# The sums of a windowed softmax: from ScalarE's exponentials to one VectorE reduction over each block

## The chip, the cores and the metric

The kernel runs on one core of a Trainium2 chip. The metric is the device time of one execution, in microseconds (us).

## The reference

Two blocks follow each other on a state of 4 x 1024 tokens of 128 channels. This case is about the second half of the first block: six layers, each a local attention (16 heads of 64, windows of 32 tokens that look back one window) and a feed-forward part. Cut to the attention:

```python
q = q * cos * scale + rotate_half(q) * sin * scale
k = k * cos * inv + rotate_half(k) * sin * inv
...
sim = jnp.einsum('bhwie,bhwje->bhwij', bq, bk2) * QK_SCALE
sim = jnp.where(mask, -jnp.finfo(sim.dtype).max, sim)
attn = jax.nn.softmax(sim, -1)
out = jnp.einsum('bhwij,bhwje->bhwie', attn, bv2)
```

For each token and head the softmax runs over 64 keys. Before this stage stand a full attention with another score function, behind it a recurrence and a mixture of experts; the change touches neither.

## The kernel before, in words

`local_layers` works through 96 units (6 layers x 16 units of 256 tokens), pipelined over several steps: in one step each engine does pieces of up to six units, `at(1)` (the youngest) to `at(6)`. Every engine has its own fixed list of calls in a function `step`, written out by hand, and runs it in order; engines meet through semaphores only. The steady part is a loop whose body holds two steps (`for odd in range(2)`), so units come in pairs; I call the step that ends in the loop's jump and what follows it the odd one, the other the even one.

A unit has two blocks of 128 tokens, x = 0 and x = 1. For a block, with tokens on the 128 partitions, the steps are:

- `scores` (PE, L775 and L782) writes 16 heads x 64 keys to a PSUM pair, the mask among them.
- `maxima` (DVE, L1148) takes the maximum of each head, and `loc_ebias` (L1150) turns it into the bias of the exponential.
- `exponentials(x, hp)` (ACT, L990) has one ACTIVATE for each of 8 heads, 128x64, with a bias and a scale from SBUF, and writes `loc_probs`. Its `accum_out` adds up the 64 numbers of a head into `loc_total`. There are four such groups of eight in a unit.
- `reciprocals(x)` (DVE, L1157) forms `loc_recip` = 1/`loc_total`, 128x16.
- `probs_across`, `probs_out`, `weighted`, `outputs` (PE L804, ACT L1008, PE L819, DVE L1166) transpose, multiply by the values and scale by `loc_recip`.

Around these lie the rotary products (`rotate_cos` L1090 and `rotate_sin` L1099 on DVE, after ACT's squares L972; the halves of `loc_msin` are swapped by DMAs that SP issues, and POOL adds them, L691, into `loc_ks` and `loc_qr`), the norms of the heads (`norms`, `norms_out` L979, `norms_across` L757, `norms_in` L1108, and `newton`, ten small operations of DVE on lines 91 to 95 that make `loc_rnorm`), the spreading of the key norms (`widen` L1127 into `loc_rk_wide`, `spread` PE L765, `scale_keys` DVE L1138), and the second half's LayerNorm (`centre` L1187, `ln_squares` ACT L1022, `ln_var` PE L854, `ln_rstd` DVE L1195 and again lines 91 to 95, `ln_spread` PE L862).

DVE's list for a step, where it matters here: `norms_in`, `reciprocals(0)`, `newton`, `rotate_cos(0)`, `widen(0)`, `rotate_sin(0)`, ..., `maxima(0, 0)`, `reciprocals(1)`, `scale_keys(1)`, and in the next step `maxima(0, 1)`, `centre`, `outputs(1)`, `ln_rstd`. ACT's: `norms_out`, `exponentials(1, 0)`, `square(0)`, `exponentials(1, 1)`, ..., `outputs_out(0)`, `exponentials(0, 0)`, `ln_squares`. PE's: `out_projection`, `project(1)`, `spread(0)`, `weighted(0)`. In that list of PE, `spread(0)` waits for two things: `widen(0)`, and, since it writes the PSUM pair from which `exponentials(1, 1)` read, for these exponentials. `weighted(0)` writes the pair that `rotate_sin(0)` reads. POOL's second `rotated` call of a unit follows `scale_keys(1)`.

Of the kernel before, what the change touches and what calls it, by code (L numbers as in the profile page):

```python
# [11 lines left out]
ALU = mybir.AluOpType  # L12
ACT = mybir.ActivationFunctionType
AX = mybir.AxisListType
# [38 lines left out]
def semaphores(nc, ctx, prefix):  # L53

    made = []

    def sem(name):
        made.append(ctx.enter_context(nc.semaphore(prefix + name)))
        return made[-1]

    return made, sem
# [57 lines left out]
def count(n, per=1, k=1):  # L119

    return START + per * n + k


def after(eng, sem, n, per=1, k=1):

    if not isinstance(n, int) or per * n + k > 0:
        eng.wait_ge(sem, count(n, per, k))
# [330 lines left out]
def local_layers(nc, const, t):  # L458

    ctx = ExitStack()  # L460
    with ctx:
        sb = lambda s, sh, dt=F32: ctx.enter_context(nc.sbuf_tensor("loc_" + s, sh, dt))
        pb = lambda s, sh: ctx.enter_context(nc.psum_tensor("loc_" + s, sh, F32))
        sems, sem = semaphores(nc, ctx, "loc_")
        x, ident, mean_w = const["x"], const["ident"], const["mean_w"]
# [22 lines left out]
        rnorm = [sb(f"rnorm{i}", [P, 2, 2 * HEADS]) for i in range(2)]  # L488
        rk_wide = sb("rk_wide", [P, HEADS * DH])
        mx, ebias, total, recip = ([sb(f"{s}{i}", [P, HEADS]) for i in range(2)] for s in ("mx", "ebias", "total", "recip"))  # L490
        probs = [sb(f"probs{i}", [P, PAIRS, 2, 2 * WIN]) for i in range(2)]
# [23 lines left out]
        mx_ready, ebias_ready, exp_ready, recip_ready = sem("mx_ready"), sem("ebias_ready"), sem("exp_ready"), sem("recip_ready")  # L515
# [3 lines left out]
        mean_ps, xc_ready, lsq_ready, var_ps, rstd_ready = sem("mean_ps"), sem("xc_ready"), sem("lsq_ready"), sem("var_ps"), sem("rstd_ready")  # L519
        lnspread_ps, xn_ready, h_ready = sem("lnspread_ps"), sem("xn_ready"), sem("h_ready")  # L520
        ff_ps, gelu_ready, hidden_ready, y_ps, xa_done = sem("ff_ps"), sem("gelu_ready"), sem("hidden_ready"), sem("y_ps"), sem("xa_done")
        fpar_ready = sem("fpar_ready")
        links, nlinks, vlinks = sem("links"), sem("nlinks"), sem("vlinks")
        passed = sem("passed")
        block = ctx.enter_context(nc.Block())
# [431 lines left out]
        def _(act):  # L957
# [23 lines left out]
            def exponentials(x, hp, u, b):  # L981
                if u is None:
                    return
                after(act, ebias_ready, u.n, 4, 2 * x + hp + 1)
                if hp == 0:
                    after(act, probsT_ps, u.n - 1, 2, x + 1)
                    after(act, recip_ready, u.n - 1, 2, x + 1)
                for p in range(PAIRS):
                    k, head = PAIRS * hp + p, HEADS + 2 * p + hp
                    ins = nc.scalar.activation(probs[x][:, p, hp, :], pairs[b][:, hp, p * 2 * WIN:(p + 1) * 2 * WIN], ACT.Exp, bias=ebias[x][:, k:k + 1],  # L990
                                               scale=rnorm[u.odd][:, x, head:head + 1], accum_out=total[x][:, k:k + 1])
                ins.then_inc(exp_ready, 1)

            def values_out(x, u, b):
# [44 lines left out]
            def step(at):  # L1039
                ln_squares(at(5))  # L1040
                square(2, at(2), 2)
                exponentials(0, 1, at(3), 1)
                values_out(0, at(3), 0)
                h_out(at(5))
                outputs_out(1, at(4), 1)
                gelus(0, at(5), 4)
                probs_out(0, at(3), 0)
                square(3, at(2), 1)
                values_out(1, at(3), 0)
                norms_out(at(2), 4)  # L1050
                exponentials(1, 0, at(3), 2)
                square(0, at(1), 1)
                exponentials(1, 1, at(3), 2)
                gelus(1, at(5), 3)
                square(1, at(1), 0)
                probs_out(1, at(3), 2)
                gelus(2, at(5), 3)
                outputs_out(0, at(3), 2)
                exponentials(0, 0, at(2), 1)
# [4 lines left out]
        def _(dve):  # L1064
# [88 lines left out]
            def reciprocals(x, u):  # L1153
                if u is None:
                    return
                after(dve, exp_ready, u.n, 4, 2 * x + 2)
                nc.vector.reciprocal(recip[x][:, :], total[x][:, :]).then_inc(recip_ready, 1)  # L1157

            def outputs(x, u, b):
# [65 lines left out]
            def step(at):  # L1225
# [13 lines left out]
                rotate_sin(3, at(2), 1)  # L1239
                norms_in(at(2), 4)  # L1240
                reciprocals(0, at(3))
                newton(at(2))
                rotate_cos(0, at(1), 1)
# [8 lines left out]
                widen(1, at(2))  # L1252
                maxima(0, 0, at(2), 1)
                reciprocals(1, at(3))
                scale_keys(1, at(2), 0)

# [358 lines left out]
def kernel_program(nc, t, out, phases=5):  # L1615
    ctx = ExitStack()
    with ctx:
        sb = lambda s, sh, dt=F32: ctx.enter_context(nc.sbuf_tensor(s, sh, dt))
        const = {
            "x": sb("x", [P, TOK]), "ident": sb("ident", [P, P]), "mean_w": sb("mean_w", [P, P]),  # L1620
            "mod": sb("mod", [P, 2 * 6 * BATCH]),
        }
        prepare(nc, const, t)
        if phases >= 1:
            theta_attention(nc, const, t)
        if phases >= 2:
            local_layers(nc, const, t)
        if phases >= 3:
            rwkv(nc, const, t)
        if phases >= 4:  # L1630
            mixture(nc, const, t, out)
        else:
            store(nc, const, out)
# [87 lines left out]
```

## Time and profile before

| | us |
|---|---|
| three runs | 5411.45, 5433.7, 5434.81 (median 5433.7) |
| the profiled execution, its own time | 5389.72 |
| its span, first to last instruction | 5387.8 |
| PE busy in the span | 4167.7 (77%) |
| DVE busy | 3552.1 (66%) |
| ACT busy | 3140.0 (58%) |
| POOL busy | 1080.8 (20%) |

The profiled execution took 5389.72 us, 0.8% less than the median of the three others; sums are made against it. The local layers take up about 81% of the span (560 to 4920 us). Busy shares say only that no engine is full; the pace comes from who waits for whom inside a step.

### The profile page before, as it was taken

The page shows a single profiled execution, that of the slowest core. Times are in us where ns is not written, and L with a number is a line of the kernel's source. Part 1 is how long each engine was busy: PE and PEld are TensorE (multiplying, and loading weights), DVE is VectorE, ACT ScalarE, POOL GpSimd, SP SyncE. Part 2 cuts the span into 40 slices and gives each one's busy share as a digit, 9 for nine tenths or more (in the row PEclk, how much of TensorE's full clock was granted, in tenths as well). Part 3 has the DMA queues.
Part 4 walks back from the last instruction along what each step waited for, and adds up shares of the span by engine and source line. Part 5 has one row for each costly group of instructions (what it writes and reads, how often), then busy time and mean ns, then how long its engine had stood idle before and what let it go on. Part 6 is the DMA issues. An engine that isn't in the chain of part 4 may idle for free. (4 is left out here: it accounts for less than half of the span.)

```text
span 5387.8 us, 176120 instructions
## 1 busy us (share of the span) xinstructions
PE 4167.7 (77%) x68250; PEld 2955.4 (55%) x68250; DVE 3552.1 (66%) x6841; ACT 3140.0 (58%) x8480; POOL 1080.8 (20%) x856
## 2 busy tenths in 40 slices
PE   5665688888888888888888888888888888885358
PEld 3443465555655656565556565556565656563124
DVE  4454576677676766676766677766766767774655
ACT  3332466666666766666666666666666666673123
POOL 0000222222222222222222222222222222220011
PEclk9776899999999999999999999999999999997579
DMA  0001233323333333333333333333333333330000
GB/s 24 0 0 38 68 77 71 73 69 89 76 72 72 73 79 82 72 72 70 81 77 77 73 72 73 84 81 72 69 72 81 85 72 74 71 81 11 0 9 12
DMA packets 138485, 337.32 MB, mean 63 GB/s; under 512 B 44880, under 2 KB 46032, under 8 KB 137552
## 3 DMA queue, kind: packets, MB, share of 16 engines
q1 hardware_dynamic: 137808, 326.67, 25.8%
q8 instruction: 622, 10.19, 0.9%
q14 instruction: 55, 0.45, 0.0%
HBM read 22.41 MB, written 2.10 MB: 5 GB/s over the span
## 5 line engine op out<-in xcount | busy, mean ns | idle before, releaser
L990 ACT ACTIVATE loc_probs<-loc_pair,loc_ebias,loc_rnorm 128x64 f32<-128x64 f32 x3072 | 1198.7, 428 | 13.4 <-DVE loc_ebias L1150 11.0
L738 PE MATMUL loc_pair<-loc_hs,loc_wqk 128*128 128x256 f32 x3072 | 795.5, 405 | 155.6 <-issue 152.3
L691 POOL TENSOR_TENSOR loc_ks<-loc_mcos,loc_swapped 128x1024 f32<-128x1024 f32 x192 | 452.1, 2355 | 1833.2 <-DVE loc_kr L1138 1345.6
L738 PEld LDWEIGHTS loc_pair<-loc_hs,loc_wqk 128*128 128x128 f32 x3072 | 589.3, 199 | 271.8 <-issue 170.6
L691 POOL TENSOR_TENSOR loc_qr<-loc_mcos,loc_swapped 128x1024 f32<-128x1024 f32 x192 | 452.6, 2357 | 1387.2 <-DMA loc_swapped<-loc_msin 1316.0
L990 ACT ACTIVATION_READ_ACCUMULATOR loc_probs<-loc_pair,loc_ebias,loc_rnorm 128x1 f32 x3072 | 704.5, 229 | 0.0
L1090 DVE SCALAR_TENSOR_TENSOR loc_mcos<-loc_pair,loc_scal,loc_tab 128x1024 f32<-128x1024 f32 x384 | 491.1, 1279 | 189.7 <-ACT loc_sq L972 170.0
L972 ACT ACTIVATE loc_sq<-loc_pair 128x1024 f32<-128x1024 f32 x384 | 395.8, 1031 | 336.1 <-PE loc_pair L738 336.1
L1148 DVE TENSOR_REDUCE loc_mx<-loc_pair 128x8 f32<-128x512 f32 x384 | 264.5, 689 | 466.6 <-PE loc_pair L782 458.4
L1099 DVE SCALAR_TENSOR_TENSOR loc_msin<-loc_pair,loc_scal,loc_tab 128x1024 f32<-128x1024 f32 x384 | 490.0, 1276 | 28.7 <-DMA loc_swapped<-loc_msin 27.4
L1001 ACT ACTIVATE loc_vodd<-loc_pair 128x1024 f32<-128x1024 f32 x192 | 196.9, 1026 | 410.4 <-DMA loc_veven<-loc_vodd 286.8
L782 PE MATMUL loc_pair<-loc_kr,loc_qr 64*32 64x64 f32 x24576 | 320.4, 226 | 137.7 <-issue 137.7
L782 PEld LDWEIGHTS loc_pair<-loc_kr,loc_qr 64*32 64x32 f32 x24576 | 272.1, 106 | 238.9 <-issue 236.2
L795 PE MATMUL loc_pair<-loc_wv,loc_hs 128*64 128x512 f32 x1536 | 401.8, 647 | 1.6 <-DVE loc_o L1166 1.4
L1166 DVE TENSOR_TENSOR loc_o<-loc_pair,loc_recip 128x512 f32<-128x512 f32 x384 | 246.3, 682 | 232.1 <-PE loc_pair L819 232.1
L819 PE MATMUL loc_pair<-loc_veven,loc_probsT 64*32 64x64 f32 x12288 | 315.3, 235 | 89.5 <-issue 82.0
L1008 ACT ACTIVATE loc_probsT<-loc_pair 128x1024 f32<-128x1024 f32 x192 | 195.9, 1020 | 317.4 <-PE loc_pair L804 317.4
L872 PE MATMUL loc_one<-loc_h,loc_w 128*128 128x256 f32 (+1 forms) x1152 | 330.2, 411 | 31.7 <-ACT loc_h L1029 22.9
L819 PEld LDWEIGHTS loc_pair<-loc_veven,loc_probsT 64*32 64x32 f32 x12288 | 272.1, 109 | 148.3 <-issue 147.8
L839 PE MATMUL loc_one<-loc_oT,loc_wo 128*128 128x256 f32 x1536 | 350.1, 381 | 0.8 <-DVE loc_act_out L1211 0.4
L1015 ACT ACTIVATE loc_oT<-loc_pair 128x1024 f32<-128x1024 f32 x192 | 195.2, 1017 | 253.9 <-PE loc_pair L829 253.9
L1150 DVE SCALAR_TENSOR_TENSOR loc_ebias<-loc_mx,loc_rnorm 128x8 f32<-128x8 f32 x384 | 313.0, 815 | 13.2
(244 smaller groups left out, 7503.6 us busy)
## 6 DMA issues: line engine op xcount, KB each, us to landing
loc_swapped<-loc_msin SPq DMA_DIRECT2D x1536, 128.0 KB, 2.3
loc_veven<-loc_vodd SPq DMA_DIRECT2D x768, 64.0 KB, 2.0
loc_veven<-loc_vodd SPq DMA_DIRECT2D x384, 128.0 KB, 2.3
loc_wqk<-wqk_dram SPq DMA_DIRECT2D x12, 512.0 KB, 3.6
loc_wv<-wv_dram SPq DMA_DIRECT2D x6, 512.0 KB, 3.6
loc_wo<-wo_dram SPq DMA_DIRECT2D x6, 512.0 KB, 4.4
x<-xT_dram SPq DMA_DIRECT2D x1, 2048.0 KB, 7.4
loc_tab<-tables_dram SPq DMA_DIRECT2D x1, 2048.0 KB, 7.7
```

The lines of the kernel that those rows point to most:

```text
L691: nc.gpsimd.tensor_tensor(dst, mcos[i % 2][:, :], swapped[:, :], ALU.add).then_inc(rope_add, 1)
L738: ins = nc.tensor.matmul(pairs[b][:, p // 2, (p % 2) * UNIT:(p % 2 + 1) * UNIT], wqk[:, k, w:w + P], hs[u.odd][:, :], start=True, stop=True)
L782: ins = nc.tensor.matmul(pairs[b][WIN * w:WIN * w + WIN, hp, p * 2 * WIN:(p + 1) * 2 * WIN], qr[u.odd][part, p, at:at + WIN], kr[u.odd][pa ...
L795: ins = nc.tensor.matmul(pairs[b][hp * DH:(hp + 1) * DH, g, :], hs[u.odd][:, BLK * x + DH * g:BLK * x + DH * g + DH], wv[:, hp, :], start= ...
L819: ins = nc.tensor.matmul(pairs[b][WIN * w:WIN * w + WIN, hp, p * DH:(p + 1) * DH], probsT[part, p, WIN * w:WIN * w + WIN], v[part, w // 2, ...
L839: ins = nc.tensor.matmul(bank(b)[:, 0:UNIT], wo[:, p, :], oT[:, p, :], start=p == 0, stop=p == PAIRS - 1)
L872: ins = nc.tensor.matmul(bank(b)[0:FB[j], k * UNIT:(k + 1) * UNIT], w1[:, at:at + FB[j]], h[:, :], start=True, stop=True)
L972: nc.scalar.activation(sq[:, i, :], flat(b), ACT.Square).then_inc(sq_ready, 1)
L990: ins = nc.scalar.activation(probs[x][:, p, hp, :], pairs[b][:, hp, p * 2 * WIN:(p + 1) * 2 * WIN], ACT.Exp, bias=ebias[x][:, k:k + 1], sc ...
L1090: nc.vector.scalar_tensor_tensor(mcos[i % 2][:, :].rearrange("p (g t) -> p g t", g=4), flat(b).rearrange("p (g t) -> p g t", g=4), scal[u. ...
L1099: nc.vector.scalar_tensor_tensor(msin[:, :].rearrange("p (g t) -> p g t", g=4), flat(b).rearrange("p (g t) -> p g t", g=4), scal[u.odd][:, ...
L1150: nc.vector.scalar_tensor_tensor(ebias[x][:, k], mx[x][:, k], -1.0, rnorm[u.odd][:, x, HEADS:].rearrange("p (g y) -> p y g", y=2)[:, hp, : ...
```

## The change

The exponentials lose `accum_out`. `reciprocals(x)` first adds up `loc_probs` of the block, 128 partitions x 16 heads x 64, with one `tensor_reduce` of DVE into `loc_total`, waits for it by a new semaphore, and then takes the reciprocals. The wait of `exponentials(x, 0)` for the reciprocals of the unit before falls away.

```diff
@@ exponentials
                 if hp == 0:
                     after(act, probsT_ps, u.n - 1, 2, x + 1)
-                    after(act, recip_ready, u.n - 1, 2, x + 1)
                 for p in range(PAIRS):
                     k, head = PAIRS * hp + p, HEADS + 2 * p + hp
                     ins = nc.scalar.activation(probs[x][:, p, hp, :], pairs[b][:, hp, p * 2 * WIN:(p + 1) * 2 * WIN], ACT.Exp, bias=ebias[x][:, k:k + 1],
-                                               scale=rnorm[u.odd][:, x, head:head + 1], accum_out=total[x][:, k:k + 1])
+                                               scale=rnorm[u.odd][:, x, head:head + 1])
                 ins.then_inc(exp_ready, 1)
@@ reciprocals
                 after(dve, exp_ready, u.n, 4, 2 * x + 2)
+                nc.vector.tensor_reduce(total[x][:, :].rearrange("t (y g) -> t g y", y=2), probs[x][:, :, :, :], AX.X, ALU.add).then_inc(sum_ready, 1)
+                dve.wait_ge(sum_ready, count(u.n, 2, x + 1))
                 nc.vector.reciprocal(recip[x][:, :], total[x][:, :]).then_inc(recip_ready, 1)
```

On DVE, in the middle of a step, the reciprocals of block 0 stand between the reading of the norms and the ten operations of `newton`. Before:

```order
620 L1108 TENSOR_SCALAR loc_norm<-loc_one 128x4x4x2 x2
621 L1157 RECIPROCAL loc_recip<-loc_total 128x16
622 L91 TENSOR_SCALAR loc_rnorm<-loc_norm 128x64
623 L76 ISA
624 L93 SCALAR_TENSOR_TENSOR loc_ntmp<-loc_rnorm,loc_norm 128x64
```

and in the changed kernel (a line added and one taken away above make the numbers of some lines differ by one):

```order
628 L1107 TENSOR_SCALAR loc_norm<-loc_one 128x4x4x2 x2
629 L1156 TENSOR_REDUCE loc_total<-loc_probs 128x8x2
630 L1158 RECIPROCAL loc_recip<-loc_total 128x16
631 L91 TENSOR_SCALAR loc_rnorm<-loc_norm 128x64
632 L76 ISA
633 L93 SCALAR_TENSOR_TENSOR loc_ntmp<-loc_rnorm,loc_norm 128x64
```

The reduction stands ahead of `newton`, and all of `newton` moves back behind it. At the end of a step, between `maxima(0, 0)` and `scale_keys(1)`, the order before is this; there the reduction comes in ahead of L1157 in the same way, and ahead of `scale_keys(1)` (L1138):

```order
664 L1148 TENSOR_REDUCE loc_mx<-loc_pair 128x8
665 L1150 SCALAR_TENSOR_TENSOR loc_ebias<-loc_mx,loc_rnorm 128x8
666 L1157 RECIPROCAL loc_recip<-loc_total 128x16
667 L127 REGISTER_ALU
668 L1138 TENSOR_TENSOR loc_kr<-loc_ks,loc_pair 128x8x128
```

ACT's order stays; each of its exponentials writes one tile where it wrote two. Before, around the two groups of block 1 (first row) and the gelu behind them:

```order
273 L990 ACTIVATE loc_probs,loc_total<-loc_pair,loc_ebias,loc_rnorm 128x64 x16
274 L1036 ACT_TABLE_LOAD
275 L1036 ACTIVATE loc_gelu<-loc_one,loc_fpar 128x256
```

and now:

```order
273 L989 ACTIVATE loc_probs<-loc_pair,loc_ebias,loc_rnorm 128x64 x16
274 L1035 ACT_TABLE_LOAD
275 L1035 ACTIVATE loc_gelu<-loc_one,loc_fpar 128x256
```

No instruction of ACT changes its place.

## Rows read from the trace of the kernel before

**Rows 1.** The page's costliest groups: the exponentials and their accumulator reads (count, busy us, mean ns)

```profile
L990 ACT ACTIVATE loc_probs<-loc_pair,loc_ebias,loc_rnorm 128x64 f32<-128x64 f32 x3072 | 1198.7, 428 | 13.4 <-DVE loc_ebias L1150 11.0
...
L990 ACT ACTIVATION_READ_ACCUMULATOR loc_probs<-loc_pair,loc_ebias,loc_rnorm 128x1 f32 x3072 | 704.5, 229 | 0.0
```

**Rows 2.** Timeline of ACT, an even unit: start, duration, what

```profile
2548.60 0.40 ACT L990 ACTIVATE loc_probs<-loc_pair,loc_ebias,loc_rnorm 128x64 f32<-128x64 f32 x1
2548.90 0.19 ACT L990 ACTIVATION_READ_ACCUMULATOR loc_probs<-loc_pair,loc_ebias,loc_rnorm 128x1 f32 x1
2549.00 0.39 ACT L990 ACTIVATE loc_probs<-loc_pair,loc_ebias,loc_rnorm 128x64 f32<-128x64 f32 x1
```

**Rows 3.** Groups of instructions on DVE, shapes apart

```profile
L94 DVE TENSOR_TENSOR loc_ntmp<-loc_ntmp,loc_rnorm 128x64 f32<-128x64 f32 x288 | 82.1, 285 | 9.9
...
L442 DVE TENSOR_REDUCE att_mx<-att_theta 128x1 f32<-128x1024 f32 x32 | 39.0, 1220 | 1.1
```

**Rows 4.** PE's waits, 1000 to 4500 us: us in total, times, longest

```profile
PE loc_pair L765 <- ACT loc_probs L990: 58.4, 57, 1.1
PE loc_one L862 <- DVE loc_rstd L95: 55.3, 36, 2.3
PE loc_one L854 <- ACT loc_lsq L1022: 50.9, 39, 1.4
```

**Rows 5.** Timeline of DVE, the even unit of [rows 2]

```profile
2548.48 0.25 DVE L1157 RECIPROCAL loc_recip<-loc_total 128x16 f32<-128x16 f32 x1
...
2550.89 0.23 DVE L95 SCALAR_TENSOR_TENSOR loc_rnorm<-loc_ntmp,loc_rnorm 128x64 f32<-128x64 f32 x1
2552.95 1.28 DVE L1090 SCALAR_TENSOR_TENSOR loc_mcos<-loc_pair,loc_scal,loc_tab 128x1024 f32<-128x1024 f32 x1 [1.83 <-ACT loc_sq L972]
...
2554.75 1.28 DVE L1099 SCALAR_TENSOR_TENSOR loc_msin<-loc_pair,loc_scal,loc_tab 128x1024 f32<-128x1024 f32 x1
```

**Rows 6.** Timeline of POOL: the middle of an odd step, then of the even one

```profile
2505.69 2.36 POOL L691 TENSOR_TENSOR loc_qr<-loc_mcos,loc_swapped 128x1024 f32<-128x1024 f32 x1 [8.18 <-DMA loc_swapped<-loc_msin]
...
2551.01 2.36 POOL L691 TENSOR_TENSOR loc_qr<-loc_mcos,loc_swapped 128x1024 f32<-128x1024 f32 x1 [4.87 <-DMA loc_swapped<-loc_msin]
```

**Rows 7.** Timeline of POOL and DVE, another even unit

```profile
1465.04 2.35 POOL L691 TENSOR_TENSOR loc_qr<-loc_mcos,loc_swapped 128x1024 f32<-128x1024 f32 x1 [4.61 <-DMA loc_swapped<-loc_msin]
1465.17 2.30 DVE L95 SCALAR_TENSOR_TENSOR loc_rnorm<-loc_ntmp,loc_rnorm 128x64 f32<-128x64 f32 x1
```

**Rows 8.** Timeline of PE: five waits in a pair of units

```profile
2508.66 1.09 PE L765 MATMUL loc_pair<-ident,loc_rk_wide 128*128 128x128 f32 x8 [0.93 <-DVE loc_rk_wide L1127]
...
2531.72 0.43 PE L862 MATMUL loc_one<-ident,loc_rstd 128*128 128x128 f32 x2 [0.86 <-DVE loc_rstd L95]
...
2555.93 1.09 PE L765 MATMUL loc_pair<-ident,loc_rk_wide 128*128 128x128 f32 x8 [0.91 <-ACT loc_probs L990]
...
2559.10 0.24 PE L819 MATMUL loc_pair<-loc_veven,loc_probsT 64*32 64x64 f32 x1 [0.71 <-issue]
...
2572.24 0.61 PE L854 MATMUL loc_one<-mean_w,loc_lsq 128*128 128x1 f32 x4 [1.41 <-ACT loc_lsq L1022]
```

**Rows 9.** Timeline of DVE, the odd unit of [rows 6]

```profile
2506.85 1.75 DVE L1127 COPY loc_rk_wide<-loc_rnorm 128x1024 f32<-128x1024 f32 x1
...
2518.41 1.22 DVE L1138 TENSOR_TENSOR loc_kr<-loc_ks,loc_pair 128x1024 f32<-128x1024 f32 x1 [0.28 <-PE loc_pair L765]
...
2528.64 0.90 DVE L91 TENSOR_SCALAR loc_rstd<-loc_var 128x2 int32<-128x2 int32 x1
```

**Rows 10.** Timeline of POOL, behind the end of the odd unit's step

```profile
2527.16 2.35 POOL L691 TENSOR_TENSOR loc_ks<-loc_mcos,loc_swapped 128x1024 f32<-128x1024 f32 x1 [4.87 <-DMA loc_swapped<-loc_msin]
```

**Rows 11.** Timeline of DVE, the end of the even unit's step

```profile
2567.22 1.22 DVE L1138 TENSOR_TENSOR loc_kr<-loc_ks,loc_pair 128x1024 f32<-128x1024 f32 x1 [0.64 <-PE loc_pair L765]
...
2569.07 1.93 DVE L1150 SCALAR_TENSOR_TENSOR loc_ebias<-loc_mx,loc_rnorm 128x8 f32<-128x8 f32 x1
2570.92 0.41 DVE L1187 TENSOR_TENSOR loc_xc<-loc_xb,loc_one 128x256 f32<-128x256 f32 x1
```

More of the change, by code:

```diff
@@ L521, in local_layers @@
         ff_ps, gelu_ready, hidden_ready, y_ps, xa_done = sem("ff_ps"), sem("gelu_ready"), sem("hidden_ready"), sem("y_ps"), sem("xa_done")
-        fpar_ready = sem("fpar_ready")
+        fpar_ready, sum_ready = sem("fpar_ready"), sem("sum_ready")
         links, nlinks, vlinks = sem("links"), sem("nlinks"), sem("vlinks")
```

## The prediction

> **What bounds the kernel now.** I read the page first: PE is the busiest engine, but with pauses, and the exponentials and the reads of their accumulators head ACT's list [rows 1]. 3072 exponentials at 32 a unit are 96 units. Then I read PE's waits, since no engine is full and the pace is that of the engine that everybody follows. Over 3500 us, some 77 units, the waits that this change can touch are three [rows 4]: `spread(0)` (L765) waits 58.4 us for the exponentials that still read its PSUM pair, `ln_spread` (L862) waits 55.3 us for the LayerNorm's Newton steps, `ln_var` (L854) waits 50.9 us for the squares. The sum is 165 us, 2.1 us a unit and 4.7% of that time, so the removal of 700 us of accumulator reads cannot show in full. The timelines of ACT, DVE and POOL around these three waits say who is late for each, and the rest of this text stays there.
>
> **ACT: what is taken off.** An accumulator read lasts 229 ns in the mean [rows 1], but it starts 0.30 us after its ACTIVATE began and the next ACTIVATE starts 0.10 us after it [rows 2]: they overlap. Without it I expect the next ACTIVATE where the read stood, so 0.10 us for each, 0.8 us for a group of eight, about 3.1 us a unit, 0.3 ms of ACT time in all. Bounds: nothing, if an ACTIVATE needs its 0.40 us of pitch anyway, and 0.23 us each, the read's whole duration. The value in between is read from two starts, so I trust it. The Trainium skill, ScalarE: Activation LUTs, What ACT_TABLE_LOAD costs, gives 186 ns plus 93 ns for each pointer operand plus 0.833 ns a column, less 93 ns of overlap back to back, which would be an estimate of 0.33 us of pitch and a gain of 0.07 us instead of 0.10; the duration that it gives, 425 ns, agrees with the row's 428.
>
> **DVE: what is added.** 192 reductions of 128x1024. The nearest row is the reduction of the same size in the stage before, 1.22 us [rows 3]; with the step to the reciprocal that now waits for it, about 1.25 us, 240 us in all. Bounds: 1.1 and 1.5 us; the 16 heads of 64 could cost a little at each head's end.
>
> **Middle of a step.** In the even unit L1157 starts at 2548.48, the last operation of `newton` ends at 2551.12, and DVE then waits 1.83 us for ACT's squares before L1090 [rows 5]. The reduction seems to fit into this pause, all the more since the squares come 0.8 us earlier behind a shorter group. But POOL starts a sum at 2551.01 [rows 6], and another even unit shows what happens when `newton` is still running then: POOL starts at 1465.04, the operation of DVE that starts at 1465.17 takes 2.30 us in place of 0.23 and ends when POOL's ends [rows 7]. The mean of L94 on `loc_ntmp`, 285 ns for an operation that mostly takes 0.23, says that this is rare now: 288 x 0.055 us is 16 us, seven or eight catches of 2.1 us on this line. With 1.25 us put ahead of it, `newton` in this even unit would run from 2549.9 to 2552.4, so half of it falls behind POOL's start. Its sixth operation is in flight at 2551.1, or held until 2553.4, and four more follow at 0.26 us: end at 2554.5. L1090 comes at 2554.4 in place of 2552.95, and L1099 at 2556.2 in place of 2554.75. PE's `spread(0)` needs L1127, ready at 2556.3, and starts at 2556.4 in place of 2555.93 [rows 8], although the exponentials for which it waited now are done 1.6 us earlier. `weighted(0)` needs L1099's end, 2557.5: it starts at about 2557.7 where it could start at 2556.95 before, 0.75 us later. What ACT gives is lost here, since DVE, which was not late, becomes late. POOL's start varies against this step by some tenths, and in many units L1108 comes earlier than here, so I take 0.6 us for an even unit. Bounds: 0.8, and 0, since PE stops inside `weighted(0)` for 0.71 us with no releaser [rows 8], and if what it waits for there (its next code) doesn't come later too, this pause takes up the delay.
>
> The rule that bears on the reduction itself is in the Trainium skill, GPSIMD Engine Reference, Specifications: GpSimd and VectorE share SBUF interfaces, with contention for DVE instructions in a two-port mode or with two SBUF inputs. By it the reduction, with one SBUF input, isn't held and `newton` is; the trace agrees for `newton` [rows 7], and no row shows a reduction beside POOL. Were it held as well, nothing would change here, for at 2548.5 to 2549.7 POOL is idle.
>
> In the odd unit POOL starts later against the step, at 2505.69, and `newton`, which ended near 2503.8, ends near 2505.1: just free. L1127 is held by POOL there (1.75 us for a copy of 0.68) until POOL ends [rows 9, 6], and PE's `spread(0)` waits for it [rows 8]. An earlier start of that copy changes nothing while POOL ends when it does. I take -0.1 us for an odd unit.
>
> **End of a step.** The reduction also stands ahead of `scale_keys(1)`. In the even unit L1138 had waited 0.64 us for PE [rows 11], so it comes 0.6 us later. POOL's next sum waits for it, L1150 is held by that sum (1.93 us) and moves along, and L1187 ends at 2571.9 in place of 2571.33 [rows 11]. The squares L1022 came at 2571.74 behind `exponentials(0, 0)`, 0.5 us before PE's L854 at 2572.24 [rows 8]. Now the exponentials are done 0.8 us earlier and the centred rows 0.6 us later: L1022 starts at about 2571.9, 0.15 us late. In the odd unit L1138 had only 0.28 us of pause [rows 9], so it comes 1.0 us later, and with it the sum of POOL that waits for it and, after a swap by DMA, the next one, at 2527.16 [rows 10]. This one holds the LayerNorm's first Newton step: L91 at 2528.64 takes 0.90 us [rows 9]. Moved to 2528.1 it holds L91 until 2530.5, and PE's L862, which waits 0.86 us there [rows 8], waits 0.9 us longer. In units in which that sum started late already it would slide behind all ten steps (2 us) and the wait, 1.5 us in the mean (55.3 us in 36) [rows 4], would go. Between +0.9 and -1.5 I take +0.25, nearer to the unit I read, in which the sum would have to move 2.5 us to be out of the way.
>
> **The sum.** For a pair: 0.6 - 0.1 + 0.15 + 0.25 = 0.9 us. 48 pairs, of which about 45 run with all stages full: 40 us, 0.75%. On the profiled execution's own 5389.7 us that is 5430. The median of the three runs is 0.8% above that execution; with the same ratio it becomes 5474, and I give 5470. The PSUM and semaphore parts of the edit cost nothing: `exponentials(x, 0)` drops a wait that was long fulfilled, since its wait for `loc_ebias` stands behind the reciprocals in DVE's order.
>
> **Rivals.** *The sums are hidden and ACT's gain counts.* If POOL's sum came after `newton` in even units, `spread(0)` would start 0.9 us earlier (its whole wait, [rows 8]): -0.9 - 0.1 + 0.15 + 0.25 = -0.6 us a pair, -27 us, 5407. It decides at a start of POOL 1.4 us later against the step than in [rows 6]. Chance 0.10. *The LayerNorm slips free.* The odd unit's POOL sum moves behind the Newton steps in most units: at -1.5 us in four of five odd units and +0.9 in the rest, -1.0 us, a pair gets 0.6 - 0.1 + 0.15 - 1.0 = -0.35 us, -16 us, and with the first delay absorbed -0.95 us, -43 us: 5390 to 5418. It decides where this sum starts more than 1.8 us behind L91. For it, the 2.3 us of the longest wait [rows 4]; against it, L91's row. Chance 0.12. *Nothing to be measured.* PE's pause in `weighted(0)` takes up the 0.6 us: 0.3 us a pair, 13 us, 5447. Chance 0.22. *The odd unit is caught too.* `newton` ends at 2505.1 against POOL's 2505.69, 0.6 us of room; if reductions take 1.5 us or POOL comes earlier, L1090 and PE's `weighted(0)` come 0.6 us later there as well: 1.6 us a pair, 72 us, 5506. Chance 0.12. The forecast itself has 0.44.
>
> **How the numbers follow.** About 0.5% is what a measurement of this kernel can tell from no change. The forecast's own range, from 0.4 to 1.3 us a pair, is 5450 to 5493, and a third of it lies within 0.5%. Slower by over 0.5%: 0.30 + 0.12 + a little of the third rival, 0.45. Within: 0.35. Faster by over 0.5%: the first two where they go far, 0.20. The range for 8 in 10 reaches to 5405 below, into the faster cases, and to 5520 above, past the catch in both units.
>
> **What would show it.** ACTIVATE to ACTIVATE on the exponentials 0.29 to 0.30 us, and no accumulator read. The reduction at 1.2 us. L93, L94 and L95 on `loc_rnorm` and `loc_ntmp` with a mean near 0.3 to 0.5 us, one operation of 2.2 us in nearly every even unit; PE's L765 waiting for DVE in place of ACT; L1090 without its wait for the squares there. L862's wait longer, L854's about the same. I'm wrong if the step is bound elsewhere: if PE's waits without a releaser shrink by what I add, if POOL's sums move against `newton`, or if `ln_spread` loses its wait.

## The result and the profile after

| | before | after |
|---|---|---|
| median of the runs, us | 5434.26 (5411.45 to 5437.28, 4 runs) | 5551.59 (5537.94 to 5557.66, 4 runs) |
| the profiled execution, its own time | 5389.72 | 5537.94 |
| DVE busy | 3552.1 | 3922.8 |
| ACT busy | 3140.0 | 2868.5 |

The ratio is 1.0222, with an interval of 1.0188 to 1.0256: slower by 2.2%, where 0.7% had been forecast, and above the range. In the profiled executions the difference is 148 us, 3.1 us for each of the 48 pairs; the forecast's sum was 0.9.

Groups of instructions (count | busy us, mean ns | idle before, releaser), beside [rows 1] and [rows 3]:

```profile
L989 ACT ACTIVATE loc_probs<-loc_pair,loc_ebias,loc_rnorm 128x64 f32<-128x64 f32 x3072 | 952.7, 431 | 12.1 <-DVE loc_ebias L1149 9.8
...
L1156 DVE TENSOR_REDUCE loc_total<-loc_probs 128x16 f32<-128x1024 f32 x192 | 233.8, 1217 | 3.3
...
L94 DVE TENSOR_TENSOR loc_ntmp<-loc_ntmp,loc_rnorm 128x64 f32<-128x64 f32 x288 | 133.3, 463 | 9.9
L93 DVE SCALAR_TENSOR_TENSOR loc_ntmp<-loc_rnorm,loc_norm 128x64 f32<-128x64 f32 x288 | 96.9, 336 | 9.9
...
L95 DVE SCALAR_TENSOR_TENSOR loc_rnorm<-loc_ntmp,loc_rnorm 128x64 f32<-128x64 f32 x288 | 90.1, 313 | 9.9
```

The group of 3072 accumulator reads is gone, and the exponentials last as long as before each (431 ns, 428 before). The reductions cost 234 us of DVE. The three kinds of `newton` step are the same instructions as before, and L94 went from 285 to 463 ns in the mean: that is time in which they were held.

PE's waits from 1000 to 4500 us (us in total, times, longest), beside [rows 4]:

```profile
PE loc_pair L738 <- issue: 111.7, 37, 3.5
PE loc_pair L782 <- issue: 105.2, 70, 2.2
PE loc_pair L765 <- DVE loc_rk_wide L1126: 98.7, 98, 1.6
PE loc_pair L819 <- issue: 96.2, 58, 2.8
PE loc_one L862 <- DVE loc_rstd L95: 81.3, 37, 2.4
...
PE loc_one L854 <- ACT loc_lsq L1021: 57.9, 37, 1.6
```

`spread(0)` (L765) waited 58.4 us for ACT's exponentials and 24.6 for DVE, 83.0 together; it now waits 98.7 us, all for DVE. `ln_spread` (L862) waits 81.3 us where it waited 55.3. The pauses without a releaser inside `weighted(0)` (L819) were 70.5 us in 54 before and are 96.2 in 58.

The middle of a step, the even unit, in the timelines (start, duration, what, idle before): ACT, DVE, POOL, PE.

```profile
2712.18 2.52 ACT L989 ACTIVATE loc_probs<-loc_pair,loc_ebias,loc_rnorm 128x64 f32<-128x64 f32 x8
```

```profile
2708.50 1.22 DVE L1156 TENSOR_REDUCE loc_total<-loc_probs 128x16 f32<-128x1024 f32 x1
2709.75 0.25 DVE L1158 RECIPROCAL loc_recip<-loc_total 128x16 f32<-128x16 f32 x1
...
2711.12 2.42 DVE L94 TENSOR_TENSOR loc_ntmp<-loc_ntmp,loc_rnorm 128x64 f32<-128x64 f32 x1
...
2714.73 1.28 DVE L1089 SCALAR_TENSOR_TENSOR loc_mcos<-loc_pair,loc_scal,loc_tab 128x1024 f32<-128x1024 f32 x1 [0.15 <-issue]
2715.93 0.68 DVE L1126 COPY loc_rk_wide<-loc_rnorm 128x1024 f32<-128x1024 f32 x1
2716.53 1.28 DVE L1098 SCALAR_TENSOR_TENSOR loc_msin<-loc_pair,loc_scal,loc_tab 128x1024 f32<-128x1024 f32 x1
```

```profile
2711.10 2.36 POOL L691 TENSOR_TENSOR loc_qr<-loc_mcos,loc_swapped 128x1024 f32<-128x1024 f32 x1 [5.95 <-DMA loc_swapped<-loc_msin]
```

```profile
2716.67 1.09 PE L765 MATMUL loc_pair<-ident,loc_rk_wide 128*128 128x128 f32 x8 [1.47 <-DVE loc_rk_wide L1126]
...
2718.06 0.25 PE L819 MATMUL loc_pair<-loc_veven,loc_probsT 64*32 64x64 f32 x2 [0.30 <-DVE loc_msin L1098]
...
2721.95 0.24 PE L819 MATMUL loc_pair<-loc_veven,loc_probsT 64*32 64x64 f32 x1 [2.42 <-issue]
```

Eight exponentials take 2.5 us, about 0.3 us apiece from start to start (0.290 in the mean of all, 0.382 before), as forecast from [rows 2]; 0.33, the other estimate there, was too high. The reduction and the reciprocal put L94's second pass at 2711.12, just behind the start of POOL's sum at 2711.10, and that 0.23 us operation lasts 2.42. L1089 has lost its wait for the squares (1.83 us in [rows 5]), because it is late itself. All of that the prediction named. What it did not name is the last row: PE starts `weighted(0)` at 2718.06, stops near its end and resumes at 2721.95, after 2.42 us; the same pause was 0.71 us in [rows 8]. That was a short one: over 40 even units the pauses of L819 come to 1.64 us a unit before and 2.26 after.

The end of the odd unit's step, DVE, POOL and then PE, beside [rows 8 to 10]:

```profile
2783.76 2.22 DVE L95 SCALAR_TENSOR_TENSOR loc_rstd<-loc_vtmp,loc_rstd 128x2 f32<-128x2 f32 x1
```

```profile
2783.61 2.35 POOL L691 TENSOR_TENSOR loc_ks<-loc_mcos,loc_swapped 128x1024 f32<-128x1024 f32 x1 [5.60 <-DMA loc_swapped<-loc_msin]
```

```profile
2786.99 0.43 PE L862 MATMUL loc_one<-ident,loc_rstd 128*128 128x128 f32 x2 [2.31 <-DVE loc_rstd L95]
```

One Newton step of the LayerNorm is held for a whole sum of POOL, and `ln_spread` waits 2.31 us, where the unit shown before had a hold of 0.9 us and a wait of 0.86.

One unit can mislead, so I averaged the starts of some instructions over 40 even and 40 odd units of each trace, counted from the start of ACT's copy of the norms (L979). Times in us:

| | even: length | `newton` ends | L1098 starts (`rotate_sin(0)`) | `weighted(0)` starts / its last matmul | `ln_spread` | odd: length | `weighted(0)` starts | `scale_keys(1)` | `ln_spread` |
|---|---|---|---|---|---|---|---|---|---|
| before | 43.73 | 4.29 | 7.89 | 10.05 / 13.30 | 30.91 | 46.80 | 10.31 | 18.64 | 32.13 |
| after | 45.47 | 7.39 | 9.34 | 10.87 / 14.73 | 32.63 | 48.23 | 10.43 | 20.00 | 33.12 |
| `reciprocals(0)` early | 43.38 | 3.97 | 7.32 | 8.90 / 12.57 | 30.61 | 46.96 | 9.84 | 19.15 | 32.32 |
| both moved | 42.08 | 4.27 | 7.37 | 8.95 / 12.58 | 29.19 | 46.27 | 9.69 | 18.11 | 31.37 |
| both moved, accumulators kept | 43.69 | 4.19 | 7.89 | 10.05 / 13.26 | 30.94 | 46.66 | 10.26 | 18.49 | 31.86 |

The last three rows are experiments below. A pair got 1.74 + 1.43 = 3.2 us longer. In the even unit `weighted(0)` starts 0.82 us later, close to what I had worked out (0.75), but its last matmul comes 1.43 us later.

### The profile page after: what moved, and what is told of

It reads as the page before. It is cut to its first block and busy times, and to the rows that moved or that the text cites. A ratio compares the mean times of both kernels' runs of the same rounds, so it can differ in the third digit from the quotient of the medians.

```text
span 5536.0 us, 173241 instructions
## 1 busy us (share of the span) xinstructions
PE 4208.0 (76%) x68250; PEld 2977.0 (54%) x68250; DVE 3922.8 (71%) x7033; ACT 2868.5 (52%) x5408; POOL 1083.0 (20%) x856
## 5 line engine op out<-in xcount | busy, mean ns | idle before, releaser
L989 ACT ACTIVATE loc_probs<-loc_pair,loc_ebias,loc_rnorm 128x64 f32<-128x64 f32 x3072 | 952.7, 431 | 12.1 <-DVE loc_ebias L1149 9.8
L1089 DVE SCALAR_TENSOR_TENSOR loc_mcos<-loc_pair,loc_scal,loc_tab 128x1024 f32<-128x1024 f32 x384 | 490.8, 1278 | 44.6 <-issue 20.7
L1098 DVE SCALAR_TENSOR_TENSOR loc_msin<-loc_pair,loc_scal,loc_tab 128x1024 f32<-128x1024 f32 x384 | 489.9, 1276 | 37.1 <-DMA loc_swapped<-loc_msin 37.0
L819 PE MATMUL loc_pair<-loc_veven,loc_probsT 64*32 64x64 f32 x12288 | 313.8, 234 | 143.5 <-issue 115.6
L819 PEld LDWEIGHTS loc_pair<-loc_veven,loc_probsT 64*32 64x32 f32 x12288 | 271.6, 109 | 196.5 <-issue 196.5
L872 PE MATMUL loc_one<-loc_h,loc_w 128*128 128x256 f32 (+1 forms) x1152 | 342.9, 424 | 21.3 <-ACT loc_h L1028 13.8
L1149 DVE SCALAR_TENSOR_TENSOR loc_ebias<-loc_mx,loc_rnorm 128x8 f32<-128x8 f32 x384 | 315.2, 821 | 13.2
L819 PE MATMUL loc_pair<-loc_vodd,loc_probsT 64*32 64x64 f32 x12288 | 318.7, 234 | 1.2 <-issue 1.2
```

Source lines behind the costliest of these rows:

```text
L819: ins = nc.tensor.matmul(pairs[b][WIN * w:WIN * w + WIN, hp, p * DH:(p + 1) * DH], probsT[part, p, WIN * w:WIN * w + WIN], v[part, w // 2, ...
L872: ins = nc.tensor.matmul(bank(b)[0:FB[j], k * UNIT:(k + 1) * UNIT], w1[:, at:at + FB[j]], h[:, :], start=True, stop=True)
L1089: nc.vector.scalar_tensor_tensor(mcos[i % 2][:, :].rearrange("p (g t) -> p g t", g=4), flat(b).rearrange("p (g t) -> p g t", g=4), scal[u. ...
L1098: nc.vector.scalar_tensor_tensor(msin[:, :].rearrange("p (g t) -> p g t", g=4), flat(b).rearrange("p (g t) -> p g t", g=4), scal[u.odd][:, ...
L1149: nc.vector.scalar_tensor_tensor(ebias[x][:, k], mx[x][:, k], -1.0, rnorm[u.odd][:, x, HEADS:].rearrange("p (g y) -> p y g", y=2)[:, hp, : ...
```

## The experiments

Each kernel was timed beside the kernel before on the same chip. Ratios are to that kernel, with the 95% interval.

**One block alone.** Block 0, then block 1, in the new form, the other block as before.

```diff
+                    acc = {} if x == 0 else dict(accum_out=total[x][:, k:k + 1])
...
-                nc.vector.tensor_reduce(total[x]...)
+                if x == 0:
+                    nc.vector.tensor_reduce(total[x]...)
```

> Only block 0 gets the new form (the sum in the middle of a step, ahead of newton); block 1 keeps its accumulators and the wait for its reciprocals. Theory A (newton is pushed behind POOL's sum, rotate_sin(0) comes 1.4 us late in even units, and PE's weighted(0) and its code with it): this place holds most of the loss, even units about 1.6 us longer, odd ones 0.3, so 80 to 95 us above the kernel before, ratio 1.015 to 1.018, and rotate_sin(0) (L1099 after L1127) as late as in the changed kernel. Rival B (VectorE is simply too full, each 1.22 us of reduction costs the same wherever it stands): half of the 117 us, 55 to 60 us, ratio 1.011.

> Only block 1 gets the new form (the sum at the end of a step, ahead of scale_keys(1)). Theory A: scale_keys(1) and POOL's sums behind it come 0.6 to 1.4 us later, ln_spread waits 0.7 us longer in odd units, the rest is hidden: 25 to 45 us above before, ratio 1.005 to 1.008. Rival B: 55 to 60 us, ratio 1.011.

Measured: 1.0071 (1.0047 to 1.0096) for block 0 alone, 1.0050 (1.0031 to 1.0069) for block 1 alone. The first is a miss, less than either theory gave; the second is at the lower edge of theory A. With block 0 alone the even unit has nearly the whole delay at the last matmul of `weighted(0)` (14.64 on the scale of the table), but `ln_spread` comes at 31.12, only 0.2 us later than before. The two together cost 2.2% and not 1.2%. The reason can be read from the same 40 even units, between the start of `weighted(1)` and `ln_spread`. On the way PE waits for ACT's squares at `ln_var`, and these stand behind `exponentials(0, 0)`. The last column counts the units in which TensorE's granted clock was at its lower level, 1.2 in place of 2.4 GHz, for a part of the way from `ln_var` to `ln_spread`:

| means in us, even units | `weighted(0)` starts | `weighted(1)` to `ln_var` | `ln_var` to `ln_spread` | units at 1.2 GHz there |
|---|---|---|---|---|
| before | 10.05 | 2.79 | 4.51 | 17 of 40 |
| block 0 alone | 10.84 | 2.49 | 3.81 | 0 |
| block 1 alone | 9.00 | 3.08 | 5.04 | 29 |
| after | 10.87 | 3.06 | 4.50 | 16 |

With block 0 alone the shorter exponentials of block 0 let the squares come earlier, and the clock stays up behind them: 0.3 + 0.7 us come back and hide most of the caught `newton`. With block 1 alone the shorter exponentials of block 1 let `weighted(0)` start 1.05 us earlier, and that is lost again on the way to `ln_spread`: the reduction ahead of `scale_keys(1)` makes the squares late, and the clock is low in more units. With both, a reduction stands in each of the two places, and neither gain is left. So one block alone is not half of the change: it has a gain that the other block's reduction takes away. This is read from the means; no run has one block's reduction with all the accumulators kept.

**The sums without the gain.** The accumulators stay, and the reductions, in their new places, write a tile that nobody reads.

```diff
-                                               scale=rnorm[u.odd][:, x, head:head + 1])
+                                               scale=rnorm[u.odd][:, x, head:head + 1], accum_out=total[x][:, k:k + 1])
...
-                nc.vector.tensor_reduce(total[x]...)
+                nc.vector.tensor_reduce(spare[x]...)
```

> Both reductions are made, but into a tile that nobody reads; the exponentials keep their accumulators and their reads, and the reciprocals are taken of these. So the cost of the reductions alone, ACT as slow as before. Theory A: where the steps wait, DVE is late and ACT is not, so ACT's 0.1 us for each exponential was worth nothing: the same as the changed kernel within 0.3%, ratio to before 1.020 to 1.026. Rival C (ACT's gain hides part of the cost): 40 us or more above the changed kernel, ratio 1.030 or more.

Measured: 1.0195 (1.0167 to 1.0223), at the lower edge of what was expected (1.020) and not to be told from the changed kernel's 1.0222. With the reductions in these places the shorter exponentials bring nothing that can be measured.

**The gain without the sums.** No accumulators and no reductions; the reciprocals are those of a constant, so the softmax is not normalised.

> The exponentials without accumulators and no reduction at all: the reciprocals are taken of a constant, so the softmax is not normalised. ACT's gain alone. Theory A: spread(0) waited 0.9 us for the exponentials in even units, and rotate_sin(0) comes 0.7 us earlier behind the squares; even units 0.7 to 0.9 us shorter, odd ones 0.1 to 0.3: 35 to 50 us below before, ratio 0.991 to 0.994. Rival (nothing waits for ACT): within 0.3% of before.

Measured: 0.9817 (0.9791 to 0.9843), a miss: ACT's gain alone is worth twice what I expected, about 100 us. It is nearly four times the 27 us of the first rival, which let it shorten `spread(0)`'s wait in even units and nothing else. The means show more: `weighted(0)` starts 1.1 us earlier in the even unit (8.94) and 0.66 us earlier in the odd one (9.65). And further on in the even unit the two stretches of the table above are 2.49 and 3.81 us, as with block 0 alone, in none of 40 units at the lower clock: 0.3 us less of waiting for the squares, and 0.7 us that the clock gives back.

**`reciprocals(0)` out of `newton`'s way.** It goes seven calls up, to where DVE waits for PE anyway.

```diff
+                reciprocals(0, at(3))
                 maxima(1, 0, at(3), 2)
...
-                reciprocals(0, at(3))
                 newton(at(2))
```

> The changed kernel with one call moved: reciprocals(0), with its sum, stands ahead of maxima(1, 0) in the same step, where DVE waits 3 to 5 us for PE, in place of ahead of newton. Both reductions are made. Theory A (newton pushed behind POOL's sum): newton ends near 4.3 us in even units again, rotate_sin(0) at 7.4, weighted(0) at 9.0, as in the run without a sum of block 0; with the end of the step left as it is, ratio to before 0.996 to 1.006, so 85 to 140 us below the changed kernel. Rival B (DVE's busy time as such): no more than 0.3% from the changed kernel, ratio 1.019 to 1.025.

Measured: 1.0023 (1.0005 to 1.0041), as expected. The reduction is the same, DVE has as much work, and 2.0% is back. `newton` ends at 3.97 us in place of 7.39, and the last matmul of `weighted(0)` comes 2.2 us earlier than after the change.

**And `reciprocals(1)` just ahead of its use.** As above, with the second reduction in the next step.

```diff
+                reciprocals(1, at(4))
                 outputs(1, at(4), 0)
...
-                reciprocals(1, at(3))
                 scale_keys(1, at(2), 0)
```

> As the run before, and reciprocals(1) moved too: from ahead of scale_keys(1) to the next step, ahead of outputs(1), so that scale_keys(1) and POOL's sums come as early as in the kernel before. Theory A: both delays are gone and ACT's gain stays, ratio 0.985 to 0.995, near the 0.982 of the run without sums; outputs(1) comes 1.2 us later in even units, and the LayerNorm's Newton steps behind it may meet POOL's sum there, which takes some of it back. Rival B: ratio 1.019 to 1.025.

Measured: 1.0249 (1.0212 to 1.0287), 3% off my expectation and no faster than the change itself. Its even unit, DVE, then POOL:

```profile
2706.81 1.20 DVE L1156 TENSOR_REDUCE loc_total<-loc_probs 128x16 f32<-128x1024 f32 x1
...
2709.76 0.15 DVE L1196 TENSOR_SCALAR loc_var<-loc_one 128x2 f32<-128x2 f32 x1
...
2711.32 2.21 DVE L93 SCALAR_TENSOR_TENSOR loc_vtmp<-loc_rstd,loc_var 128x2 f32<-128x2 f32 x1
```

```profile
2711.16 2.34 POOL L691 TENSOR_TENSOR loc_ks<-loc_mcos,loc_swapped 128x1024 f32<-128x1024 f32 x1 [4.89 <-DMA loc_swapped<-loc_msin]
```

`scale_keys(1)` was earlier, so POOL's next sum but one was earlier too, and the LayerNorm's Newton steps, moved back by the reduction, ran into it in even units, where they had been free. PE's L862 shows it (1000 to 4500 us):

```profile
PE loc_one L862 <- DVE loc_rstd L95: 133.2, 72, 2.7
```

It is the same mechanism at another place, and I had looked only at the place I wanted to clear.

**POOL's sum made short.** The direct test of the hold: the sum of POOL that catches `newton` adds up 64 columns in place of 1024 inside the loop, so a part of the rotated queries is not computed. It was done to the kernel before and to the changed one.

```diff
-                nc.gpsimd.tensor_tensor(dst, mcos[i % 2][:, :], swapped[:, :], ALU.add)...
+                if i == 3 and not isinstance(u.n, int):
+                    nc.gpsimd.tensor_tensor(dst[:, 0:64], mcos[i % 2][:, 0:64], swapped[:, 0:64], ALU.add)...
```

> The kernel before, with POOL's fourth sum of a unit (the one that starts 4 to 6 us into a step) cut to 64 of its 1024 columns in the loop, so that most of the second half of loc_qr is old data: the sum lasts 0.2 to 0.3 us in place of 2.35. It is the base for the next run. widen(0) is no longer held in odd units. Both theories: 0 to 1.0% below before.

> The changed kernel with the same cut of POOL's fourth sum. Theory A (the lock of POOL's sum makes the middle sum expensive): newton ends at 5.2 us in even units in place of 7.4, rotate_sin(0) starts at 7.2 in place of 9.3, weighted(0) at 9.0 to 9.3: the loss of the middle place is gone, the ratio of this run to the one before is 1.005 or less. Rival (newton is late by the reduction's own 1.25 us and the rest is PE's): the ratio between the two stays at 1.015 or more.

Measured: 0.9961 (0.9944 to 0.9977) and 0.9958 (0.9939 to 0.9977). With POOL's instruction short, the change costs nothing, although `newton` still ends 1.3 us later in the even unit than with the same cut in the kernel before (5.25 against 3.96). Groups of the second kernel (its lines stand three further down):

```profile
L94 DVE TENSOR_TENSOR loc_ntmp<-loc_ntmp,loc_rnorm 128x64 f32<-128x64 f32 x288 | 65.3, 227 | 9.9
...
L692 POOL TENSOR_TENSOR loc_qr<-loc_mcos,loc_swapped 128x64 f32<-128x64 f32 x90 | 29.8, 331 | 615.9 <-DMA loc_swapped<-loc_msin 615.9
```

L94 is back at 227 ns with the reduction still ahead of it. So the loss of 2.2% needs the hold by one 2.36 us instruction of another engine; the reduction's own 1.2 us ahead of `newton` is not enough for it. ACT's gain doesn't show there either: with the reduction still ahead of `scale_keys(1)` the two stretches of the even unit are 2.89 and 4.67 us, 2.76 and 4.26 with the same cut in the kernel before.

**The reductions where they push nothing into POOL's sum.** The two placements above, the one that helped and the one that missed, say what a place must do: not delay an operation into a sum of POOL that holds it. `reciprocals(1)` goes behind `scale_keys(1)`, which starts POOL's sum; there `maxima(0, 1)` ends in L1149, held by that sum for 1.9 us anyway. Three kernels: with `reciprocals(0)` ahead of `maxima(1, 0)`, with it in its place of the change, and with it ahead of `norms_in`.

```diff
+                reciprocals(1, at(4))
                 maxima(0, 1, at(3), 1)
...
-                reciprocals(1, at(3))
                 scale_keys(1, at(2), 0)
```

> The changed kernel with reciprocals(0) ahead of maxima(1, 0), as in the earlier run, and reciprocals(1) moved behind scale_keys(1), ahead of maxima(0, 1) of the next step. Theory A (what matters is where DVE stands against POOL's sums; a reduction reads one SBUF operand and isn't held): scale_keys(1) comes 1.4 us earlier in both units, POOL's sum behind it too, and the reduction runs while that sum holds the GpSimd-shared operations, in time that the step of L1149 (1.9 us for 0.17) loses anyway. 0.5 to 1.0 us a unit less than with reciprocals(0) moved alone: 0.985 to 0.995 of the kernel before. Rival B (a reduction is held by POOL as well): the reduction lasts over 2 us and nothing is won against the kernel with reciprocals(0) moved alone: 1.000 to 1.005. Rival C (the LayerNorm's Newton steps meet the next sum, as when reciprocals(1) stood ahead of outputs(1)): 1.01 to 1.03.

> The changed kernel with reciprocals(1) alone moved behind scale_keys(1), ahead of maxima(0, 1) of the next step; reciprocals(0) stays ahead of newton. Theory A: the catch of newton and the longer pause in weighted(0) stay (1.4 us in an even unit), the end of the step gets back what the reduction cost there and 0.5 us more: 1.003 to 1.012 of the kernel before. Rival B (reduction held): 1.02. Rival C (Newton steps of the LayerNorm meet the next sum): 1.02 to 1.04.

> As the first of these, but reciprocals(0) stands ahead of norms_in, a place before its place in the change, where DVE waits 1.4 us for PE's norms anyway. Theory A (newton only has to start at its old time): within 0.4% of the kernel with reciprocals(0) ahead of maxima(1, 0), so 0.985 to 0.998 of the kernel before, newton ending at its old 4.0 to 4.5 us behind ACT's copy of the norms. Rival: norms_in slips by several tenths because exponentials end late against the norms, newton is caught in part, 1.005 to 1.012.

Measured: 0.9797 (0.9761 to 0.9833), 1.0035 (1.0015 to 1.0054) and 0.9801 (0.9775 to 0.9826). The first and the third are 2% faster than the kernel before, with every operation of the changed kernel in them, and faster than theory A had it (0.985 at best). The second is inside theory A, at its lower end: `newton` is still caught (it ends at 7.32 us) and `weighted(0)` has its last matmul at 14.60, but `ln_spread` comes at 31.02, for the two stretches behind are 2.50 and 3.81 us again. The ratios by place:

| | `reciprocals(1)` ahead of `scale_keys(1)` | behind it |
|---|---|---|
| `reciprocals(0)` ahead of `newton` | 1.0222 | 1.0035 |
| `reciprocals(0)` ahead of `maxima(1, 0)` | 1.0023 | 0.9797 |

Either move gives back about 2%, whether the other is made or not.

In the first of the three `scale_keys(1)` came only 0.5 us earlier in the even unit and 1.0 in the odd one than with `reciprocals(0)` moved alone, not 1.4; the gain is larger further on, at `ln_spread` (1.4 and 0.95 us, from the table). In the even unit that is the two stretches once more, 3.00 and 4.71 us with `reciprocals(0)` moved alone, 2.47 and 3.81 here. Of the first, the start of a step, DVE then POOL:

```profile
2650.30 1.22 DVE L1137 TENSOR_TENSOR loc_kr<-loc_ks,loc_pair 128x1024 f32<-128x1024 f32 x1 [0.45 <-PE loc_pair L765]
2651.43 1.21 DVE L1156 TENSOR_REDUCE loc_total<-loc_probs 128x16 f32<-128x1024 f32 x1
...
2653.71 0.36 DVE L1149 SCALAR_TENSOR_TENSOR loc_ebias<-loc_mx,loc_rnorm 128x8 f32<-128x8 f32 x1
```

```profile
2651.70 2.34 POOL L691 TENSOR_TENSOR loc_ks<-loc_mcos,loc_swapped 128x1024 f32<-128x1024 f32 x1 [12.05 <-DVE loc_kr L1137]
```

The reduction runs beside POOL's sum and takes its 1.21 us. L1149, 1.93 us in [rows 11], takes 0.36. In the groups and in PE's waits (1000 to 4500 us) of the same kernel:

```profile
L1149 DVE SCALAR_TENSOR_TENSOR loc_ebias<-loc_mx,loc_rnorm 128x8 f32<-128x8 f32 x384 | 165.6, 431 | 13.1
```

```profile
PE loc_one L862 <- DVE loc_rstd L95: 47.2, 34, 2.3
PE loc_one L854 <- ACT loc_lsq L1021: 39.2, 40, 1.1
...
PE loc_pair L765 <- DVE loc_rk_wide L1126: 21.8, 35, 1.3
```

After the change L1149 was 315.2 us, 821 ns in the mean; half of it is gone. L765 waits 21.8 us (98.7 after the change, 83.0 before) and L862 47.2.

**Is that gain ACT's or that of the places?** The fastest kernel with the accumulators put back.

> The fastest kernel so far (reciprocals(0) ahead of maxima(1, 0), reciprocals(1) behind scale_keys(1)) with the accumulators put back: the exponentials write loc_total as before, the reductions stay where they are and write a spare tile. Theory A (with the sums out of the way of POOL's instructions ACT's shorter groups are worth what they were with no sums at all, about 1.8%): 0.995 to 1.003 of the kernel before, about 2% above the fastest kernel. Rival: the gain comes from the new places of the reciprocals themselves, and the accumulators cost next to nothing, as they did where the reductions stood in newton's way: 0.978 to 0.985.

Measured: 1.0011 (0.9989 to 1.0033), theory A to the point. PE's waits of this kernel, 1000 to 4500 us:

```profile
PE loc_pair L765 <- ACT loc_probs L990: 63.3, 62, 1.1
PE loc_one L862 <- DVE loc_rstd L95: 57.0, 35, 2.3
PE loc_one L854 <- ACT loc_lsq L1022: 50.2, 38, 1.4
```

They are close to those of [rows 4] again. So with these places the reductions are free, and the shorter exponentials are worth 2.1% (1.0011 against 0.9797); with the reductions in the places of the change they were worth nothing (1.0195 against 1.0222).

## Why the prediction was wrong

The mechanism, the sign and the places were right, and the runs show them; that is not luck. Two terms of the sum were far too small: the middle of the even step, 0.6 us taken and 1.43 measured, and the end of the odd step, 0.25 taken and about 1.3 measured.

- **What ACT gives.** 0.09 us for each exponential (0.382 to 0.290 us from start to start) where 0.10 was priced, none of it showing. That it would show only where DVE isn't late held too, but the first rival priced it far too low, at 27 us; it is 100 us with no sums, and 108 with the sums in better places. That rival left out the squares at `ln_var` and the clock behind them.
- **What DVE adds.** Held: 1.217 us against 1.22 taken.
- **The even middle, 0.6 us taken.** I had L1099 1.45 us late and `weighted(0)` 0.75 us late, and took the second, less a little, as what passes on. The means are 1.45 (7.89 to 9.34) and 0.82 (10.05 to 10.87), as worked out. But the pause without a releaser inside `weighted(0)`, which I took as constant or as absorbing, grew. Its last matmul comes 5.41 us behind the start of `rotate_sin(0)` before and 5.39 after, and 5.1 to 5.4 in all the other kernels: it follows `rotate_sin(0)`, not the start of `weighted(0)`. So 1.43 us came through. The fetch of instructions that ends this pause starts 2.7 us behind the start of `rotate_sin(0)` before and 2.6 after, which is 0.5 and 1.1 us behind the start of `weighted(0)`. Why it follows `rotate_sin(0)` stays open. PE's wait for that operation can be what lets the fetch be asked for; but the swap DMAs of `loc_msin` start 2.70 us behind it too, in both kernels, and no run tells the two apart.
- **The odd middle, -0.1 us taken.** `weighted(0)` starts 0.12 us later. `newton` had the 0.6 us of room that I read, or a little less: its end moves by 1.7 us in the mean and not by 1.3, so some odd units are caught, a small part of the fourth rival.
- **The end of the odd step, 0.25 us taken.** In microseconds this term missed by most. `scale_keys(1)` is 1.36 us later (1.0 worked out) and `ln_spread` 1.0 us later. I had worked out 0.9 for the unit I read and taken 0.25, because units in which POOL's sum slid behind the Newton steps might gain. None of that gain shows: L862's waits grew from 55.3 to 81.3 us. The averaging towards a benefit that no row showed was the error. Another 0.4 us comes behind `ln_spread`, most of it in PE's wait for DVE at `norms` (L748, 0.27 us an odd unit before and 0.56 after), which no term of the sum had.
- **The end of the even step, 0.15 us taken.** The unit is 1.74 us longer, 1.43 of it by the end of `weighted(0)`. The 0.3 that is left is the wait for the squares (2.79 to 3.06 us in the first table of the experiments), which I had said would stay about the same.

With 1.43 for the even middle, 0.3 for the even end and 1.43 for the odd unit the sum is 3.2 us a pair, 152 us over 48 pairs, against 148 in the profiled executions. The range ended at 5520 because its worst case added the catch in odd units to the other terms at their taken values. The upper bound of the even middle (0.8) was itself a guess about the pause.

TensorE's clock has a part in this that the prediction did not look at. From `ln_var` to `ln_spread` in the even unit PE takes 3.81 us in the mean where the clock stays at 2.4 GHz, and 5.5 where a part runs at 1.2 (in every kernel but the one with `reciprocals(1)` just ahead of its use, in which `ln_spread` waits for DVE there). That is 0.7 us an even unit before and after alike, so it is no part of the 148 us; but it is gone in the fastest kernel, and over 48 pairs that would be 34 of its 108 us, as an estimate. It was also gone with block 0 alone, which is why that kernel lost so little. With the same exception, in the kernels without it PE waits 1.0 us for the squares ahead of this stretch (L854, a mean even unit), and 1.3 to 1.6 us in those with it; no run isolates what lets the clock fall. The total says little: in the 80 units the clock was at 1.2 GHz for 287 us before, 341 after, 277 with block 0 alone, 396 with block 1 alone and 242 in the fastest kernel, and block 1 alone costs only 0.5%.

## What to carry to other kernels

Before adding an operation to an engine, list the operations behind it that another engine's long instructions hold, and find on which side of them the addition puts each: one 1.2 us reduction cost 2% or nothing, by its place alone. Put what isn't held into the time in which something else would be. An engine's gain shows only while no other engine is late for the same consumer, so price it with the rest of the change put out of the way before giving it up. And don't take half of a change for half of its cost: each half here kept a gain that the other half's addition takes away.

## What the runs showed of the hardware

- An operation of DVE that reads two tensors from SBUF waits for the end of the whole instruction that POOL has running: 0.23 us became 2.42, and with POOL's instruction cut to 0.33 us L94's mean went back to 227 ns. A column of SBUF given as a scalar doesn't count as the second: after the change 24 of the `rotate_cos` operations, with `loc_scal` and `loc_tab` from SBUF and the rest from PSUM, start inside a sum of POOL and last 1.276 us in the mean, 1.277 where no sum runs. A reduction with one SBUF operand is not held: in the fastest kernel 100 of the 192 overlap a sum of POOL by more than 0.6 us, and last 1.214 us in the mean against 1.211 for the others (counted in its trace). One operand alone is no safe conduct: the copy L1127 has one as well and is held in [rows 9]. The Trainium skill, GPSIMD Engine Reference, Specifications, names two SBUF inputs or a two-port mode as the conditions; these rows agree with the first and contradict neither.
- An accumulator read that lasts 0.19 us on the timeline costs 0.09 us of pace (0.382 against 0.290 us from one exponential to the next), eight exponentials 2.5 us in place of 3.2.
- PE pauses for its next instructions near the end of `weighted(0)`, and the last matmul behind this pause comes 5.1 to 5.4 us behind the start of `rotate_sin(0)` in the means of all the kernels, whenever `weighted(0)` itself starts; so the pause grows where `rotate_sin(0)` is later and `weighted(0)` less so (1.64 to 2.26 us an even unit). What ties it to that operation is open.
- One and the same stretch of PE, `ln_var` to `ln_spread`, takes 3.81 us in even units with the granted clock at 2.4 GHz, and 5.5 us in the mean where a part of it runs at 1.2.
